# A vision tower in float32: the first attention in one block, another order in two linear attentions, and six picks in place of seven in the graph attention

## The chip, the cores and the metric

The kernel runs on one core of one Trainium2 chip. The metric is the device time of one launch, in microseconds (us). TensorE (PE) multiplies matrices, VectorE (DVE), ScalarE (ACT) and GpSimd (POOL) work on tiles, SyncE (SP) issues most transfers; GpSimd issues the indexed ones.

## The reference

A tower of ten parts in float32 works on `h`, 128 images of 64 tokens with 64 features: a token stage of Fourier layers, then four times an attention and an expert stage, each added to its input. Four parts matter here:

```python
# L0 attention, per image (64 tokens), on n = layernorm(h)
q = n @ q_weight; h = h + sigmoid(q @ n.T) @ n
# L2 attention: linear attention with 8 heads, then a small network, two layernorms
q, k, v = split(x @ Wqkv.T); q, k = elu(q) + 1, elu(k) + 1
out = (q @ (k.T @ v)) / (q @ k.sum() + 1e-6)     # per head
y = ln(out + x, g1, b1); h = h + ln(y + gelu(y @ W1 + b1) @ W2 + b2, g2, b2)
# L3 attention: the same linear attention on rmsnorm(x), one output product
# L3 experts: a graph attention over 262144 edges and 8192 loops decides the gate:
e = leaky_relu(a_src[src] + a_dst[dst]); alpha = segment_softmax(e, dst)
agg = segment_sum(h[src] * alpha, dst)
```

## The kernel before

`h` stays in SBUF as 64 tiles of 128 tokens. The program is a chain of stages, `t.stage(...)`: each is a block in which every engine has its own list of instructions, tied by semaphores, with a barrier of all engines behind it. Within a stage an engine works strictly in the order of its list; that order is written out by hand.

**First attention** (`l0_attention`). A loop of 4 rounds of 16 tiles; a round is three stages: `norm_stage` (mean, square, root, scaling on VectorE and ScalarE), `turn_stage` (TensorE turns the tiles, ScalarE copies them to `a_xt`) and a stage with query product, scores, sigmoid, values and the add to `h`, in groups of 4 tiles. Two images share a tile, so scores are 128 x 128 of which two quarters are used; the other two quarters of `a_att` are set to zero once in a stage of their own (L864).

**Linear attentions** (`l2_attention`, `l3_attention`). One stage each over 8 chunks of 8 tiles, in steps `s`. A step works on several chunks at once: L2 normalizes chunk s+1 (a), works out the attention of chunk s, the first norm of s-1 (b) and the second of s-2 (d). A chunk has two halves (`g` = 0, 1) of 4 tiles. On TensorE: `sums` (key times value, 8 small products of 64 rows), `outs` (query times the masked sums), `turn`, `features` (query, key and value), `hidden`, `dense`. `masked` on VectorE moves sums to `a_r`, from one bank that both halves share; `divide` takes `outs`. All turned tiles and `hidden` go through one bank, each copied by ScalarE before the next. In L2 VectorE adds the dense result (`add_dense`, L1670) right after the means of the other two chunks, and one scaling, one root and one reciprocal serve all three norms.

**Graph attention** (`graph_attention`). The edges, sorted by target, lie as 128 rows of 2112 columns, in 33 chunks of 64 columns. For each column 128 rows of a table of 8192 nodes (24 numbers) are needed. 36 columns (`ASKED`) are fetched by GpSimd, one indirect DMA each (L2779, `g_g`). The other 28 (`TURNED`) are picked by TensorE: 7 picks (`PICKS`) of 4 columns, each 16 products of a one-hot matrix `g_hot` with the table in SBUF. VectorE (L2835) and ScalarE (L2807, L2811) build `g_hot` from `g_near`, which SyncE loads; VectorE multiplies the result with a mask (L2850, `g_prod`) and reduces it (L2854). `hot_near` runs two picks ahead. Once a chunk `own_scores` completes the picked columns, and VectorE waits for the gathers of the chunk (its first reader is `g_a`, L2878) and works through scans up to `g_st`; in between it takes the first pick of the next chunk. GpSimd has three buffers and waits for `st_ready` (L2911) of the chunk three back. The stage before, `graph_table`, makes the table and the `near` and `far` numbers of the picked columns; the stage behind reads the states by 64 more gathers (L2961).

```python
for c in range(CHUNKS_E):
    if c >= GB: p.wait_ge(st_ready, c - GB + 1)
    for j in range(ASKED): p.indirect_dma_start(...)   # GpSimd
```

Of the kernel before, what the change touches and what calls it, by code (L numbers as in the profile page):

```python
# [8 lines left out]
ALU = mybir.AluOpType  # L9
# [3 lines left out]
P = 128  # L13
# [782 lines left out]
def norm_stage(t, src, dst, eps, centre=True, gain=None, shift=None, add_src=False):  # L796

    nc, n = t.nc, src.shape[1]
    mean, var, tmp = t.n_mean[:, 0:n], t.n_var[:, 0:n], t.n_tmp[:, 0:n, :]
    with t.stage("own", "centred", "squared", "var_ready", "std_ready") as (block, own, centred, squared, var_ready, std_ready):  # L800
        base = dst if centre else src

        @block.vector
        def _(v):
            c = Chain(v, own)
            if centre:
                c.link(v.tensor_reduce(mean, src, AX, ALU.add))
                c.link(v.tensor_scalar(mean, mean, -1.0 / D, None, ALU.mult))
                v.tensor_tensor(dst, src, bc(mean, D), ALU.add).then_inc(centred, 1)
            v.wait_ge(squared, 1)  # L810
            c.link(v.tensor_reduce(var, tmp, AX, ALU.add))
            v.tensor_scalar(var, var, 1.0 / D, eps, ALU.mult, ALU.add).then_inc(var_ready, 1)
            v.wait_ge(std_ready, 1)
            c.link(v.reciprocal(mean, var))
            c.link(v.tensor_tensor(dst, base, bc(mean, D), ALU.mult))
            if gain is not None:
                c.link(v.tensor_tensor(dst, dst, gain.unsqueeze(1).broadcast_to([P, n, D]), ALU.mult))
            if shift is not None:
                c.link(v.tensor_tensor(dst, dst, shift.unsqueeze(1).broadcast_to([P, n, D]), ALU.add))
            if add_src:  # L820
                c.link(v.tensor_tensor(dst, dst, src, ALU.add))

        @block.scalar
        def _(act):
            if centre:
                act.wait_ge(centred, 1)
            act.activation(tmp, base, ACT.Square).then_inc(squared, 1)
            act.wait_ge(var_ready, 1)
            act.activation(var, var, ACT.Sqrt).then_inc(std_ready, 1)

def turn_stage(t, src, dst):

    nc = t.nc
    with t.stage("turned", "moved") as (block, turned, moved):
        G = src.shape[1] // GT

        @block.tensor
        def _(pe):
            for g in range(G):  # L840
                if g >= 2:
                    pe.wait_ge(moved, g - 1)
                for k in range(GT):
                    last = pe.transpose(t.bank[g % 2][0:D, k * P:(k + 1) * P], src[:, g * GT + k, :], t.ident[:, :])
                last.then_inc(turned, 1)

        @block.scalar
        def _(act):
            for g in range(G):
                act.wait_ge(turned, g + 1)  # L850
                act.activation(dst[0:D, g * 512:(g + 1) * 512], t.bank[g % 2][0:D, :], ACT.Copy).then_inc(moved, 1)

def l0_attention(t, q_w):
    nc = t.nc
    with ExitStack() as ctx:
        x = t.sb("a0_x", [P, IT, D], ctx=ctx)
        xt = t.sb("a0_xt", [D + 1, IT * P], ctx=ctx)
        qt = t.sb("a0_qt", [D, 2, 512], ctx=ctx)
        att = t.sb("a0_att", [P, 2, GT, P], ctx=ctx)  # L860
        with t.stage("z") as (block, z):
            @block.vector
            def _(v):
                v.memset(att[:], 0.0)  # L864
        with nc.Fori(0, STEPS) as it:
            h = t.h[:, bass.ds(it * IT, IT), :]
            norm_stage(t, h, x[:], 1e-5)
            turn_stage(t, x, xt)
            with t.stage("q_done", "q_moved", "s_done", "a_ready", "v_done", "h_added") as (block, q_done, q_moved, s_done, a_ready, v_done, h_added):
                @block.tensor  # L870
                def _(pe):
                    def values(g):
                        pe.wait_ge(a_ready, g + 1)
                        if g >= 2:
                            pe.wait_ge(h_added, g - 1)
                        for k in range(GT):
                            last = pe.matmul(t.bank[4 + g % 2][:, k * D:(k + 1) * D], att[:, g % 2, k, :], x[:, g * GT + k, :], start=True, stop=True)
                        last.then_inc(v_done, 1)
                    for g in range(G):
                        if g >= 2:  # L880
                            pe.wait_ge(q_moved, g - 1)
                        pe.matmul(t.bank[g % 2][0:D, :], q_w, xt[0:D, g * 512:(g + 1) * 512], start=True, stop=True).then_inc(q_done, 1)
                        pe.wait_ge(q_moved, g + 1)
                        if g >= 2:
                            pe.wait_ge(a_ready, g - 1)
# [2388 lines left out]
```

## Time and profile before

| what | us |
|---|---|
| median of 3 runs | 11217.74 (11216.36 to 11220.24) |
| the profiled execution | 11220.0 |
| its span | 11218.2 |

### The profile page before, as it was taken

To read this page: it belongs to the slowest core of one execution; us is meant where nothing else is said; L and a number is where in the kernel's file an instruction comes from. 1 tells how busy PE (TensorE), PEld (TensorE's weight loads), DVE (VectorE), ACT (ScalarE), POOL (GpSimd) and SP (SyncE) were. 2 spreads that over 40 slices of the span, in tenths; PEclk is the share of its full clock that TensorE was granted. 3 is DMA by queue.
4 is the path that set the end of the run, shared out by engine and by line. 5 is a ranking of instruction groups with operands and counts; after the bars stand their busy time and mean duration, and the time that the engine had idled before them with its cause. 6 is when DMAs were issued, how large, how long until landed. Compare 5 with 4: busy or idle time off the path is not lost. (4 is left out here: it accounts for less than half of the span.)

```text
span 11218.2 us, 158703 instructions
## 1 busy us (share of the span) xinstructions
PE 9046.3 (81%) x63076; PEld 5585.6 (50%) x63076; DVE 7150.8 (64%) x9529; ACT 4551.4 (41%) x10565; POOL 5436.7 (48%) x5545
## 2 busy tenths in 40 slices
PE   4999899899996299469788888887667599999956
PEld 3666566566654266242222222223433477777742
DVE  5878788800000589734599999993444388888863
ACT  1333333333342133223477777872333233333322
POOL 0001777777777300037655555556164376666630
PEclk7999899989998699759999999997577599999977
DMA  5000100100010000000000000000000232222210
GB/s 183 20 20 21 33 22 23 29 27 22 21 37 17 27 21 4 28 12 1 1 2 2 2 2 2 2 2 1 1 1 1 26 57 56 55 55 55 53 55 8
DMA packets 274391, 281.84 MB, mean 25 GB/s; under 512 B 203241, under 2 KB 227573, under 8 KB 267832
## 3 DMA queue, kind: packets, MB, share of 16 engines
q1 hardware_dynamic: 96344, 251.64, 6.9%
q0 software_dynamic: 177312, 20.11, 3.2%
q8 instruction: 497, 8.14, 0.3%
q14 instruction: 238, 1.95, 0.1%
HBM read 210.30 MB, written 61.06 MB: 24 GB/s over the span
## 5 line engine op out<-in xcount | busy, mean ns | idle before, releaser
L2414 POOL DMA_INDIRECT sorted<-by_row_rows,by_row_idx x2112 | 2051.3, 971 | 2758.3 <-SPq L62 1176.3
L2500 POOL DMA_INDIRECT sorted<-r_rows,r_pos x2112 | 2054.2, 973 | 1705.5 <-PE bank L597 1063.1
L2080 DVE TENSOR_TENSOR a_top<-bank,a_k 128x2048 f32<-128x2048 f32 x896 | 1972.5, 2278 | 7.8 <-ACT a_qs L2135 6.9
L2795 PE MATMUL bank<-g_tab,g_hot 128*128 128x256 f32 x7392 | 1680.8, 391 | 234.8 <-DVE g_hot L2835 130.7
L2795 PEld LDWEIGHTS bank<-g_tab,g_hot 128*128 128x128 f32 x7392 | 1448.6, 197 | 466.7 <-DVE g_hot L2835 202.4
L2779 POOL DMA_INDIRECT g_g<-table,g_el x1188 | 1184.4, 997 | 580.8 <-issue 355.0
L578 PE MATMUL bank<-f_space,f_proj 128*128 128x512 f32 x2048 | 982.1, 603 | 386.8 <-DVE f_qa L780 384.4
L2282 PE MATMUL bank<-a_top,sc_pick_row 128*32 128x512 f32 x7168 | 951.9, 615 | 307.9 <-DVE a_top L2080 292.0
L2489 DVE TENSOR_TENSOR_SCAN r_work<-r_hit,r_base 128x528 f32<-128x528 bf16 x772 | 1017.1, 1317 | 27.6
L2128 ACT ACTIVATE a_over<-a_k,a_qs 128x64 f32<-128x64 f32 x4096 | 1021.3, 337 | 0.0
L780 DVE TENSOR_TENSOR f_qa<-f_qa,bank 128x512 f32<-128x512 f32 x128 | 82.2, 683 | 1469.5 <-PE bank L587 1275.0
L597 PE MATMUL bank<-f_space,f_to_y 112*128 112x512 f32 x2048 | 967.7, 600 | 19.7 <-ACT f_space L689 19.7
L704 ACT ACTIVATE f_space<-bank,f_b1r 128x512 f32<-128x512 f32 x1024 | 647.4, 683 | 821.6 <-PE bank L597 821.6
L587 PEld LDWEIGHTS bank<-f_from_y,f_space 128*128 128x128 f32 x6144 | 747.1, 192 | 185.1 <-issue 185.1
L578 PEld LDWEIGHTS bank<-f_space,f_proj 128*128 128x128 f32 x2048 | 388.6, 192 | 864.6 <-issue 829.6
L587 PE MATMUL bank<-f_from_y,f_space 128*128 128x96 f32 x6144 | 738.4, 273 | 0.0
L1365 DVE TENSOR_TENSOR e_hid<-e_hid,bank 128x512 f32<-128x512 f32 x512 | 338.5, 684 | 539.8 <-ACT e_hid L1328 214.1
L695 ACT ACTIVATE f_space<-bank 128x384 f32<-128x384 f32 x384 | 188.2, 490 | 1184.1 <-PE bank L587 1184.1
L2850 DVE TENSOR_TENSOR g_prod<-bank,g_mask 128x512 f32<-128x512 f32 x462 | 438.0, 1025 | 339.8 <-PE bank L2795 339.8
L2807 ACT ACTIVATE g_apart<-g_near,sc_place 128x512 f32<-128x512 f32 x462 | 308.0, 713 | 774.4 <-DMA g_near<-near 412.3
L2282 PEld LDWEIGHTS bank<-a_top,sc_pick_row 128*32 128x32 f32 x7168 | 151.0, 109 | 880.5 <-DVE a_top L2080 761.1
L2491 DVE COPY_PREDICATED r_work<-r_hit,r_work 128x528 f32<-128x528 uint16 x772 | 573.6, 743 | 0.0
(574 smaller groups left out, 13449.1 us busy)
## 6 DMA issues: line engine op xcount, KB each, us to landing
f_wm<-folded SPq DMA_DIRECT2D x16, 4608.0 KB
g_near<-near SPq DMA_DIRECT2D x231, 256.0 KB, 6.7
sorted<-r_rows,r_pos POOLq DMA_INDIRECT x2112
sorted<-by_row_rows,by_row_idx POOLq DMA_INDIRECT x2112, 2.1
states<-g_st SPq DMA_DIRECT2D x33, 768.0 KB, 3.8
g_g<-table,g_el POOLq DMA_INDIRECT x1188, 2.6
fp_raw<-t_modes SPq DMA_DIRECT2D x4, 2304.0 KB, 15.1
folded<-fp_turned SPq DMA_DIRECT2D x16, 576.0 KB, 9.2
```

Source lines behind the costliest of these rows:

```text
L578: last = pe.matmul(t.bank[4 + hf][:, :], proj[:, cg].rearrange("p o y -> p (o y)"), rr[:, cg % 2 * 2 + hf, :], start=(cg == 0), stop=(cg = ...
L587: last = pe.matmul(t.bank[6 + cg % 2][:, b * 96:(b + 1) * 96], rr[:, cg % 2 * 2 + hf, b * P:(b + 1) * P], const["from_y"][:, hf * 96:(hf + ...
L597: last = pe.matmul(t.bank[cg % 2 * 2 + hf][:, :], const["to_y"][:, hf * P:(hf + 1) * P], aa[:, cg, :], start=True, stop=True)
L704: last = act.activation(rr[:, cg % 2 * 2 + hf, :], t.bank[cg % 2 * 2 + hf][:, :], ACT.Relu, bias=f.b1r[:, u % LAYERS, cg:cg + 1])
L2080: v.tensor_tensor(top[:, n % RD].rearrange("p q (h s) -> p q h s", s=S), q, kk, ALU.max).then_inc(top_done, 1)
L2128: last = act.activation(over[:, slot, q, e, :], ks[:, k % 2, e, :], ACT.Relu, scale=-1.0, bias=qs[:, k % 2, slot, at_q:at_q + 1])
L2282: last = pe.matmul(sums[k % 2][32 * q:32 * q + 32, :], t.pick_row[:, i, :], rhs, start=False, stop=(i == I16 - 1), skip_group_check=True)
L2414: p.indirect_dma_start(out=self.dst, out_offset=bass.IndirectOffsetOnAxis(ap=self.idx[:, k:k + 1], axis=0), in_=self.rows[:, k, :], in_off ...
L2489: c.link(v.tensor_tensor_scan(self.run, self.hit[:], self.hit[:], self.base[:, i:i + 1], ALU.add, ALU.bypass))
L2500: p.indirect_dma_start(out=self.dst, out_offset=bass.IndirectOffsetOnAxis(ap=self.pos[:, k // PART_STEPS, at:at + 1], axis=0), in_=self.ro ...
L2779: p.indirect_dma_start(out=g[:, c % GB, j, :], out_offset=None, in_=d["table"], in_offset=bass.IndirectOffsetOnAxis(ap=el[:, at, 0:1], axi ...
L2795: last = pe.matmul(out, hot[:, n % HB, k, j * P:(j + 1) * P], by_near[:, k, :, 0:HD * EX], start=(k == 0), stop=(k == NEAR - 1))
```

## The change

The first attention becomes one stage over 8 chunks of 8 tiles. Each engine works on chunk s+1 (norm, turning) and chunk s (scores, sigmoid, values) in one step, and the products of the two images of a tile are made apart, as 64 x 64. The zero stage, the loop and the barriers go. In a step TensorE makes the scores of chunk s (16 products), turns both halves of chunk s+1 into two banks, makes the values of chunk s (16 products) and the query product of chunk s+1. ScalarE does the square of s+1, the sigmoid of s, the root of s+1 and two copies to `xt`. VectorE does two query copies of s, mean, scaling and centring of s+1, the add to `h` of s-1, then variance, reciprocal and scaling of s+1.

In the linear attentions both halves of `outs` follow `sums` before `features`, the turning of y (L2) or z (L3) of one half stands ahead of `features` and the other behind it. On VectorE in L2 the add of the dense result and its centring move behind `finish_q`, `finish_k` of half 0 ahead of the reduces; `masked(s, 1)` and `divide(s, 0)` move forward. `finish_k` waits for the value copies as well (`va_moved`).

In the graph attention `PICKS` is 6, so `TURNED` is 24 and `ASKED` 40.

```diff
 def l0_attention(t, q_w):
-        with nc.Fori(0, STEPS) as it:
-            norm_stage(t, h, x[:], 1e-5)
-            turn_stage(t, x, xt)
-            with t.stage("q_done", "q_moved", "s_done", ...):
+    CT, CG = 8, 2
+    NC8 = TILES // CT
+        with t.stage("own", "centred", "squared", ..., "h_added"):
+            @block.tensor
+            def _(pe):
+                for s in range(-1, NC8):
+                    if has(s):
+                        pe.wait_ge(q_moved, CG * (s + 1))
+                        if s >= 1:
+                            pe.wait_ge(a_ready, s)
+                        ...
+                    if has(s + 1):
+                        pe.wait_ge(x_ready, s + 2)
+                        ...
+                    if has(s):
+                        pe.wait_ge(a_ready, s + 1)
+                        ...
+                    if has(s + 1):
+                        ...
+            @block.scalar
+            def _(act):
+                ...
+            @block.vector
+            def _(v):
+                ...
@@ l2_attention, TensorE
                         pe.wait_ge(x_ready, s + 2)
-                        for g in range(CG):
-                            turn(x, 3, s + 1, g, n + g)
+                        turn(x, 3, s + 1, 0, n)
                     if has(s):
                         outs(s, 0)
                         sums(s, 1)
+                    if has(s + 1):
+                        turn(x, 3, s + 1, 1, n + 1)
+                    if has(s):
+                        outs(s, 1)
@@
                         turn(y, 2, s - 1, 1, m + 1)
-                    if has(s):
-                        outs(s, 1)
@@ l2_attention and l3_attention, VectorE
                     v.wait_ge(ex_k_done, CG * i + g + 1)
+                    v.wait_ge(va_moved, CG * i + g + 1)
@@ l2_attention, VectorE
-                    if has(d):
-                        add_dense(d)
-                        c.link(v.tensor_reduce(mean[:, 2], z[:, d % 3], AX, ALU.add))
-                    c.link(v.tensor_scalar(mean[:, lo:hi, :], mean[:, lo:hi, :], -1.0 / D, None, ALU.mult))
+                    if lo < 2:
+                        c.link(v.tensor_scalar(mean[:, lo:min(hi, 2), :], mean[:, lo:min(hi, 2), :], -1.0 / D, None, ALU.mult))
@@
+                    if has(s):
+                        finish_q(s)
                     if has(d):
+                        add_dense(d)
+                        c.link(v.tensor_reduce(mean[:, 2], z[:, d % 3], AX, ALU.add))
+                        c.link(v.tensor_scalar(mean[:, 2], mean[:, 2], -1.0 / D, None, ALU.mult))
                         v.tensor_tensor(c_[:], z[:, d % 3], bc(mean[:, 2], D), ALU.add).then_inc(centred, 1)
                     if has(s):
-                        finish_q(s)
+                        finish_k(s, 0)
@@
                     if has(s):
-                        for g in range(CG):
-                            finish_k(s, g)
+                        finish_k(s, 1)
@@ l3_attention, TensorE
+                        sums(s, 0)
+                        outs(s, 0)
+                        sums(s, 1)
                     if has(s + 1):
                         pe.wait_ge(y_ready, s + 2)
-                        for g in range(CG):
-                            turn(y, s + 1, g, n + g)
+                        turn(y, s + 1, 0, n)
+                    if has(s):
+                        outs(s, 1)
+                    if has(s + 1):
+                        turn(y, s + 1, 1, n + 1)
+                    if has(s):
+                        pe.wait_ge(o_used, CG * s + 1)
+                        turn(z, s, 0, m)
+                    if has(s + 1):
                         features(s + 1)
                     if has(s):
-                        outs(s, 1)
-                        for g in range(CG):
-                            pe.wait_ge(o_used, CG * s + g + 1)
-                            turn(z, s, g, m + g)
+                        pe.wait_ge(o_used, CG * s + 2)
+                        turn(z, s, 1, m + 1)
                         dense(s, m + 2)
@@ graph attention
-PICKS = 7
+PICKS = 6
```

## Rows read from the trace of the kernel before

**Rows 1.** Windows: us, busy PE, PEld, DVE, ACT, POOL, granted clock, DMA share, GB/s.

```profile
...
4754.00:4925.00 171.00, 105.59 (x352) 70.06 (x352) 40.52 (x61) 41.95 (x68) 0.00 (x0) 0.52 0.00 0
...
8930.00:10820.00 1890.00, 1681.41 (x7395) 1448.84 (x7395) 1500.57 (x2713) 595.80 (x991) 1185.01 (x1189) 0.95 0.27 54
```

**Rows 2.** Timeline, graph attention, one chunk: start, us, engine, line; [idle before <-releaser].

```profile
...
9803.47 44.68 PE L2795 MATMUL bank<-g_tab,g_hot 128*128 128x256 f32 x192 [4.07 <-DVE g_hot L2835]
...
9813.65 1.92 DVE L2850 TENSOR_TENSOR g_prod<-bank,g_mask 128x512 f32<-128x512 f32 x2 [2.34 <-PE bank L2795]
...
9820.56 1.91 DVE L2850 TENSOR_TENSOR g_prod<-bank,g_mask 128x512 f32<-128x512 f32 x2 [2.81 <-PE bank L2795]
...
9840.40 0.79 DVE L2878 TENSOR_TENSOR g_a<-g_g,g_flag 128x256 f32<-128x256 f32 x1
...
9849.61 7.14 PE L2795 MATMUL bank<-g_tab,g_hot 128*128 128x256 f32 x32 [1.46 <-issue]
```

**Rows 3.** Timeline, first and last chunk's g_a, and the next stage's start.

```profile
...
8991.61 0.79 DVE L2878 TENSOR_TENSOR g_a<-g_g,g_flag 128x256 f32<-128x256 f32 x1
...
10797.78 0.79 DVE L2878 TENSOR_TENSOR g_a<-g_g,g_flag 128x256 f32<-128x256 f32 x1
...
10819.34 0.79 SPq L2954 DMA_DIRECT2D k_x<-starts  x2
```

**Rows 4.** Windows of a busy stretch in L2 and of a slow pick.

```profile
...
8042.30:8053.50 11.20, 11.11 (x76) 8.21 (x78) 4.92 (x12) 1.51 (x3) 0.00 (x0) 0.50 0.00 0
9803.50:9808.50 5.00, 5.00 (x12) 4.01 (x13) 4.93 (x7) 0.00 (x0) 3.78 (x5) 0.50 0.78 214
```

**Rows 5.** Groups by line, graph attention, GpSimd: busy, mean ns, idle before.

```profile
...
L2779 POOL DMA_INDIRECT g_g<-table,g_el x1188 | 1184.4, 997 | 580.8 <-issue 355.0 <-DVEq L2911 225.7
```

**Rows 6.** Line L2779 alone: min/median/max ns, first and last start.

```profile
...
L2779 POOL DMA_INDIRECT g_g<-table,g_el x1188: 940/944/1467, 8930.9 to 10694.8; - x198
```

**Rows 7.** Timeline, GpSimd's first wait in the graph attention.

```profile
...
9407.36 1.19 POOL L2779 DMA_INDIRECT g_g<-table,g_el  x1 [8.89 <-DVEq L2911]
```

**Rows 8.** Timeline, first attention: start, a query product and copy, end.

```profile
...
4755.78 0.91 DVE L864 MEMSET a_att<- 128x1024 f32 x1 [57.51 <-PEq L70]
...
4783.02 1.97 PE L882 MATMUL bank<-a_xt,sw_a_q 64*64 64x512 f32 x2
...
4785.03 0.68 DVE L916 COPY a_qt<-bank 64x512 f32<-64x512 f32 x1 [1.36 <-PE bank L882]
...
4923.65 0.42 DVE L911 TENSOR_TENSOR h<-h,bank 128x256 f32 x1 [1.28 <-PE bank L877]
```

**Rows 9.** Timeline, second linear attention (L2), one chunk.

```profile
...
8038.77 0.18 DVE L1701 TENSOR_SCALAR a_var<-a_var 128x24 f32<-128x24 f32 x1
...
8044.43 1.11 PE L1536 MATMUL bank<-a_va,a_k 64*64 64x65 f32 x16
...
8045.48 1.06 PE L1506 MATMUL bank<-sc_ident,a_y 128*64 128x128 f32 x4
...
8059.48 1.28 ACT L1595 ACT_TABLE_LOAD   x1
...
8060.77 0.63 ACT L1595 ACTIVATE a_ex_q<-a_low_q 128x512 f32<-128x512 f32 x1
...
8063.30 0.69 DVE L1670 TENSOR_TENSOR a_z<-bank,a_y 128x512 f32<-128x512 f32 x1 [4.39 <-PE bank L1561]
...
8071.20 1.06 PE L1506 MATMUL bank<-sc_ident,a_x 128*64 128x128 f32 x4
...
8076.08 1.06 PE L1506 MATMUL bank<-sc_ident,a_y 128*64 128x128 f32 x4
```

**Rows 10.** Timeline, last linear attention (L3): dense products of two chunks.

```profile
...
8646.87 3.67 PE L1809 MATMUL bank<-sw_a_out,a_yt 65*128 65x64 f32 x16 [0.68 <-ACT a_yt L1867]
...
8670.61 3.67 PE L1809 MATMUL bank<-sw_a_out,a_yt 65*128 65x64 f32 x16 [0.68 <-ACT a_yt L1867]
```

**Rows 11.** Timeline, a gather of the stage after the graph attention.

```profile
...
10843.01 4.91 POOL L2961 DMA_INDIRECT k_se<-states,k_end  x1 [0.30 <-issue]
```

More of the change, by code:

```diff
@@ L793, in fno @@
         return f.h
[L796 to L829, printed above, removed]
@@ L832, in turn_stage @@
[L832 to L851, printed above, removed]
@@ new lines, in _ @@
+                c = Chain(v, own)
+                for s in range(-1, NC8 + 1):
+                    a, d = s + 1, s - 1
+                    if has(s):
+                        for g in range(CG):
+                            v.wait_ge(q_done, CG * s + g + 1)
+                            if s >= 2:
+                                v.wait_ge(s_done, s - 1)
+                            v.tensor_copy(qt[:, s % 2, g * 512:(g + 1) * 512], q_bank[g][0:D, :]).then_inc(q_moved, 1)
+                    if has(a):
+                        c.link(v.tensor_reduce(mean[:], chunk_of(a), AX, ALU.add))
+                        c.link(v.tensor_scalar(mean[:], mean[:], -1.0 / D, None, ALU.mult))
+                        v.tensor_tensor(x[:, a % 3], chunk_of(a), bc(mean[:], D), ALU.add).then_inc(centred, 1)
+                    if has(d):
+                        v.wait_ge(v_done, d + 1)
+                        v.tensor_tensor(chunk_of(d), chunk_of(d), v_bank[:, :].rearrange("p (j d) -> p j d", d=D), ALU.add).then_inc(h_added, 1)
+                    if has(a):
+                        v.wait_ge(squared, a + 1)
+                        c.link(v.tensor_reduce(var[:], sq[:], AX, ALU.add))
+                        v.tensor_scalar(var[:], var[:], 1.0 / D, 1e-5, ALU.mult, ALU.add).then_inc(var_ready, 1)
+                        v.wait_ge(std_ready, a + 1)
+                        c.link(v.reciprocal(mean[:], var[:]))
+                        v.tensor_tensor(x[:, a % 3], x[:, a % 3], bc(mean[:], D), ALU.mult).then_inc(x_ready, 1)
@@ L1574, in _ @@
                         sums(s, 1)
+                    if has(s + 1):
+                        turn(x, 3, s + 1, 1, n + 1)
+                    if has(s):
+                        outs(s, 1)
                     if has(s - 1):
@@ L1581, in _ @@
                         turn(y, 2, s - 1, 1, m + 1)
-                    if has(s):
-                        outs(s, 1)
-                    if has(s - 1):
                         for g in range(CG):
@@ L1708, in _ @@
                         v.tensor_tensor(x[:, a % 3], x[:, a % 3], bc(mean[:, 0], D), ALU.mult).then_inc(x_ready, 1)
+                    if has(s):
+                        masked(s, 0)
                     if has(b):
@@ L1714, in _ @@
                         v.sem_inc(y_ready, 1)
-                    if has(s):
-                        masked(s, 0)
                     if has(d):
                         c.link(v.tensor_tensor(c_[:], c_[:], bc(mean[:, 2], D), ALU.mult))
+                    if has(s):
+                        masked(s, 1)
+                        divide(s, 0)
+                    if has(d):
                         c.link(v.tensor_tensor(c_[:], c_[:], wide(g2), ALU.mult))
@@ L1956, in _ @@
                         v.sem_inc(y_ready, 1)
+                    if has(s):
+                        masked(s, 1)
+                        divide(s, 0)
                     if has(d):
@@ L1962, in _ @@
                     if has(s):
-                        masked(s, 1)
-                        for g in range(CG):
-                            divide(s, g)
+                        divide(s, 1)
 TILE_SENDS = 18
```

117 lines of the change are left out of this document (54 added, 63 removed).

## The prediction

> **What bounds the kernel now.** One core runs a chain of stages with a barrier after each, so what a stage loses or gains is lost or gained by the whole; the change touches four. I first took time, TensorE work and granted clock of the stages by windows [rows 1]: the first attention (171 us) and the graph attention (1890 us with its start and end) are shown. The reader is to see that TensorE is busy for 105.6 of 171 us in the first at a granted clock of 0.52, that is mostly 1.2 GHz, and 1681 of 1890 us in the second at 0.95, mostly 2.4 GHz. So the graph stage looks TensorE-bound, the first attention bound by a chain.
>
> Next one chunk of the graph attention in order of time [rows 2]. A pick (4 columns, 16 products) takes 6.91 us (two ends that VectorE's multiply follows: 9813.65 and 9820.56). Seven are 48.4 us. From the first chunk's processing to the last (`g_a`, 32 chunks on) it is 1806.17 us [rows 3], 56.44 us a chunk. The other 8 us are two pauses of TensorE, 4.07 and 1.46 us, in which VectorE works through its scans and builds no one-hot rows (after the first instruction of the scans, `g_a` at 9840.40, TensorE has no new rows until 9849.61), and a slow stretch behind the longer pause: from 9803.47 to 9813.65 a pick takes 10.2 us, 3.3 too much, while the granted clock is 0.50 [rows 4]; 48.4 + 5.5 + about 2.5 on average makes 56.4.
>
> Then GpSimd in that stage [rows 5]. Its 1188 gathers hold 1184.4 us and 355.0 us lie between them as issue: 1539.4 / 1188 = 1.296 us each, 36 of them 46.7 us. It has slack: the other idle time, 225.7 us, are waits of once a chunk until VectorE frees a buffer. Before the first of them it never waited: 360 gathers from 8930.9, the start of the first [rows 6], to 9407.36 less the 8.89 us of wait [rows 7] are 467.6 us, 1.299 each.
>
> **Change 1: 6 picks in place of 7.** It removes one pick a chunk, 6.91 us of TensorE, with two multiplies, a reduce and the one-hot rows on VectorE and ScalarE, which wait for TensorE there. VectorE and TensorE together would then need 56.44 - 6.91 = 49.5 us a chunk. It adds 4 gathers a chunk: 40 x 1.299 = 52.0 us. That is more than 49.5, so GpSimd becomes the bound. What stops for it is VectorE, at the first instruction that reads gathered rows (`g_a`), some 2.5 us a chunk; behind it are the scans, the exponentials and the one-hot rows of the third pick on, so TensorE's short pause grows from 1.5 to about 4 us. I also asked whether the pause costs a second slow stretch. It may (the pause of 4.07 us does), but then the processing needs up to 49.5 + 3.3 = 52.8 us, the wait for gathers vanishes and with it the longer pause. Both lie near 52, so I take 52.0.
>
> Bounds: from below 40 x (0.94 + 0.30), the least of a gather [rows 6] and its mean gap (355.0 / 1188), 49.6 us; from above 53.5, for a slow stretch in most chunks and a late landing.
>
> The stage: chunk 0 needs its 40 gathers, 8930.9 + 40 x 1.299 + 2.6 us to land = 8985.5, where `g_a` began at 8991.61. The last begins 32 x 52.0 later, 10649.5, and from it to the next stage are 21.6 us as before [rows 3]: 10671 in place of 10819.3, **148 us less** (225 less by the lower bound, 100 by the upper). The transfers of `g_near` fall from 231 to 198, with the same five in hand; those of `near` and the preparation of the table get shorter by a seventh in places where GpSimd's 64 other gathers and a slow store set the time, so I count nothing. SyncE's stores of the states stand behind fewer loads.
>
> **Change 2: the first attention as one pipeline.** Now the stage runs from 4755.78 to the end of the last add, 4924.07 [rows 8], 168.3 us, in four rounds of three blocks with barriers. The new one has 8 chunks of 8 tiles. Its loop closes over all engines, with prices from [rows 8, 9], from the start of a chunk's query product at 0: the first copy of it at 2.0 (as 4783.02 to 4785.03), the second after another 1.8, done at 4.5; three VectorE steps of the next chunk (mean, scale, centre: 0.6 + 0.2 + 0.7) to 6.0; square 0.65 on ScalarE to 6.7; table load 1.29 for the sigmoid to 8.0; sigmoid 0.65 to 8.65; table load for the root to 9.9; root 0.2, reciprocal and scaling to 11.1 with the handovers; on TensorE two turnings of 1.0 (to 13.1), the values as 16 small products at 1.05 per 8 (to 15.1); then the next query product. The scores, the add to h and the copies to `xt` lie beside it. So **15.1 us a chunk** at 1.2 GHz. Fill (norm, turn) about 6.8, drain (copies 4.5, scores 2.2, sigmoid 0.7, values 2.1, add 0.8) 10.3: 6.8 + 7 x 15.1 + 10.3 = 122.8 in place of 168.3: **45 us less**. The memset of `a_att`, its block and the zero halves of the products go with it. Bounds: 17 us a chunk if each of some ten handovers costs 0.2 us more than I give it (30 us gained), 11.4 if all of it ran at 2.4 GHz (below).
>
> Of the table load the row says that the next instruction starts 1.29 us after the load does, 8059.48 to 8060.77 [rows 9]. The Trainium skill, "ScalarE: Activation LUTs", section "What ACT_TABLE_LOAD costs", adds a drain of about 1.38 us to each switch, 2.66 in all. By the page two loads a chunk would make the chunk 17.8 us and the gain some 22 us smaller; the rows show no such drain here, and I go by them.
>
> **Change 3: second linear attention (L2), order of outputs.** One chunk takes 30.60 us (8045.48 to 8076.08), a closed chain in three parts [rows 9]: from the add of the dense result (8063.30) to the turning of x (8071.20) 7.90; from there to the turning of y 4.88; and from that turning through features and dense back to the add 17.82. The change moves that add behind the centring of x and y and `finish_q` (three steps at 0.6 leave the part), puts one `finish_k` (0.4) before the reduces, and lets the reciprocal wait for the root alone (0.3 less): 7.90 becomes 6.2. The second part gains one group of output products (1.05) and loses a wait for ScalarE's copy (0.75): 5.3 with a little wait for the second mask. In the third the copy of y is no longer hidden by those products, and they are gone: 17.5. Together 29.0, **1.6 less in each of 6 chunks and about 1 at the ends: 11 us**. VectorE gets lows earlier and has time for all of it. The added waits on `va_moved` cost nothing: ScalarE has both copies done 0.6 us after the exponentials, ahead of the squares that the variance needs; uncovered they would be 0.6 us a chunk. Bounds 0 and 20.
>
> **Change 4: the last linear attention (L3).** The dense products of one chunk and of the next start 23.74 us apart [rows 10]. The edit swaps two waits on copies (0.7 each) for one and puts the z turning ahead of the features, yet the dense product still stands behind features, two z turnings and a copy. By my count it saves 1.5 us at 1.2 GHz, but now and then TensorE has 2.4 GHz in the features, and a shift of that pattern eats as much. I take 0.5 a chunk, **4 us**; bounds -8 and +12.
>
> **The sum.** 148 + 45 + 11 + 4 = 208 us. The profiled execution took 11220.0 us (its span 11218.2 and 1.8 around it), 2.3 over the median 11217.74: 11220.0 - 208 = 11012 for such an execution, **11010** for the median. No change can be told from one within 0.2%, 22 us.
>
> **Rivals.** *A second slow stretch (0.17).* The pause that the gathers cause is added to the slow clock, and a chunk takes 53.5 us. For it: 4.07 us of pause is followed by a slow pick. Against: the two are coupled as above. Stage 100 us less, total 11058.
>
> *Gathers cheaper than they look (0.10).* The gathers that last longer than 0.94 lie beside VectorE's work, of which there is a seventh less in the picks. At 50.5 us a chunk 48 us more are gained: 10962.
>
> *The first attention at full clock (0.13).* In the new loop turning, values and query products stand back to back for 7.6 us. At 2.4 GHz the query copies come 1.8 us earlier, the turnings and values take half: 11.4 us a chunk, 30 us more: 10980. Against it: in the second linear attention TensorE is busy for 11.11 of 11.20 us and the clock stays at 0.50 all through [rows 4], with the same small products. The Trainium skill, "TensorE: Matmul & The Clock Gate", section "Part 1: The HAM clock gate", says that activity releases a throttled clock, which speaks for this rival; by that rule the row should have shown a rise, and it shows none.
>
> *Slower: gathers blocked (0.02).* In the next stage a gather lasts 4.91 us [rows 11], in a stretch in which VectorE runs steps over 4096 elements. If more gathers meant longer ones, the stage would turn: to be 22 us slower in spite of 60 us from the attentions, `g_a` must come every (10819.3 + 82 - 21.6 - 8985.5) / 32 = 59.2 us, 1.48 us a gather. The longest of 1188 is 1.467 and half of them last 0.94 [rows 6]; so hardly.
>
> *The change does little (0.03).* At 57 us a chunk (1.43 a gather) gains and loss cancel.
>
> **How the numbers follow.** The forecast has 0.55; its own range is 10985 to 11035, from 51.5 to 52.5 us a chunk and 10 us either way in the attentions. The range takes in the rivals with the slow stretch, the cheap gathers and the full clock but for their ends: 10955 to 11065. Only the last two rivals are not faster: faster 0.95, within 0.2% 0.03, slower 0.02.
>
> **What would show it.** In the graph stage: GpSimd without any wait for VectorE, `g_a` starting every 52 us with a wait for a gather of 2 to 3 us ahead of it, TensorE at some 1440 us of work with a larger idle share; `g_a` every 49.5 us, or GpSimd still waiting for VectorE, would show that GpSimd isn't the bound. In the first attention: sigmoids 15 us apart and two table loads a chunk. In the second linear attention: features 29.0 us apart. The prediction is wrong if the gathers change their price, or if the clock does.

## The result and the profile after

The changed kernel takes 10949.4 us (median of 4 runs, 10946.2 to 10952.9) against 11217.1 (4 runs, 11214.1 to 11220.2): a ratio of 0.9767, 95% interval 0.9755 to 0.9779, 268 us less. The forecast was 11010; the measured time lies 6 us under 10955, the low end of the range that was given. The profiled execution has a span of 10946.3 us, 271.9 less than before.

Anchors that stand in both programs cut the two spans into the same stages: the load of h, the first reduce of the experts, the memset ahead of L2, the reduce of the next experts, the memset ahead of L3, the first copy of the table, the first load of the graph attention and the first of the stage behind it. From the windows between them, in us:

| stage | before | after | measured | forecast |
|---|---|---|---|---|
| first attention, load included | 198.6 | 142.0 | -56.6 | -45 |
| second linear attention (L2) | 270.1 | 227.7 | -42.4 | -11 |
| last linear attention (L3) | 215.4 | 194.8 | -20.6 | -4 |
| preparation of the table | 132.4 | 129.2 | -3.2 | 0 |
| graph attention | 1890.3 | 1736.2 | -154.1 | -148 |
| all else | 8511.4 | 8516.4 | +5.0 | 0 |

Windows of the changed kernel: first attention, L2, L3 and graph attention (columns as in [rows 1]).

```profile
4728.50:4870.50 142.00, 63.51 (x608) 39.30 (x608) 41.54 (x80) 41.45 (x56) 0.00 (x0) 0.56 0.14 47
7850.50:8078.20 227.70, 139.71 (x992) 95.50 (x992) 155.33 (x324) 93.70 (x150) 0.00 (x0) 0.61 0.00 1
8487.10:8681.90 194.80, 125.00 (x960) 97.76 (x960) 121.26 (x301) 66.76 (x122) 0.00 (x0) 0.57 0.00 1
8811.10:10547.30 1736.20, 1458.13 (x6336) 1251.22 (x6337) 1350.59 (x2545) 513.64 (x859) 1310.03 (x1321) 0.93 0.29 55
```

The column to see is the granted clock. The same windows of the kernel before have 0.52, 0.51 and 0.52 in the three attentions: there TensorE ran at 1.2 GHz nearly throughout.

Groups of the changed kernel in the graph attention, GpSimd's gathers (answers to [rows 5]), and then the line of the first instruction that reads them: min/median/max ns, first and last start, and what its engine waited for.

```profile
L2764 POOL DMA_INDIRECT g_g<-table,g_el x1320 | 1309.1, 992 | 402.3 <-issue 402.3
```

```profile
L2863 DVE TENSOR_TENSOR g_a<-g_g,g_flag x33: 786/790/793, 8866.5 to 10525.7; 128x256 f32<-128x256 f32 x33
  DMA g_g<-table,g_el: 149.7, 32
```

(1309.1 + 402.3) / 1320 = 1.2965 us a gather, and GpSimd waits for nothing but its own issue: the waits for VectorE of [rows 5] are gone. `g_a` comes every (10525.7 - 8866.5) / 32 = 51.85 us, 40 gathers of 1.2965 to the hundredth, and waits 4.7 us for them each time.

Timeline of the changed kernel in the first attention: the scaling of three chunks, and one table load with the sigmoid behind it.

```profile
4770.39 1.28 ACT L861 ACT_TABLE_LOAD   x1
4771.68 0.60 ACT L861 ACTIVATE a_att<-bank 128x512 f32<-128x512 f32 x1
...
4774.07 0.69 DVE L895 TENSOR_TENSOR a_x<-a_x,a_mean 128x512 f32<-128x512 f32 x1
4787.59 0.69 DVE L895 TENSOR_TENSOR a_x<-a_x,a_mean 128x512 f32<-128x512 f32 x1
4802.17 0.69 DVE L895 TENSOR_TENSOR a_x<-a_x,a_mean 128x512 f32<-128x512 f32 x1
```

A chunk takes 14.58 us where its query product runs at 1.2 GHz (3.62 us) and 13.1 to 13.5 us where a part of it runs at 2.4 (2.2 to 2.6 us).

### The profile page after: what moved, and what is told of

Read it like the earlier page. It is cut to its first block and busy times, and to the rows that moved or that the text cites. A ratio compares the mean times of both kernels' runs of the same rounds, so it can differ in the third digit from the quotient of the medians.

```text
span 10946.3 us, 156350 instructions
## 1 busy us (share of the span) xinstructions
PE 8748.7 (80%) x62276; PEld 5333.8 (49%) x62276; DVE 7006.8 (64%) x9390; ACT 4467.7 (41%) x10421; POOL 5559.9 (51%) x5677
## 5 line engine op out<-in xcount | busy, mean ns | idle before, releaser
L2780 PE MATMUL bank<-g_tab,g_hot 128*128 128x256 f32 x6336 | 1458.1, 394 | 298.4 <-issue 181.1
L2764 POOL DMA_INDIRECT g_g<-table,g_el x1320 | 1309.1, 992 | 402.3 <-issue 402.3
L2780 PEld LDWEIGHTS bank<-g_tab,g_hot 128*128 128x128 f32 x6336 | 1251.2, 198 | 505.1 <-issue 193.0
L597 PEld LDWEIGHTS bank<-f_space,f_to_y 112*128 112x128 f32 x2048 | 364.7, 192 | 355.1 <-issue 328.6
L560 PE MATMUL bank<-f_to_x,f_bb 96*64 96x128 f32 (+1 forms) x4096 | 507.2, 289 | 31.2 <-ACT f_bb L684 31.2
```

Of the source, the lines that this page charges most:

```text
L597: last = pe.matmul(t.bank[cg % 2 * 2 + hf][:, :], const["to_y"][:, hf * P:(hf + 1) * P], aa[:, cg, :], start=True, stop=True)
L2764: p.indirect_dma_start(out=g[:, c % GB, j, :], out_offset=None, in_=d["table"], in_offset=bass.IndirectOffsetOnAxis(ap=el[:, at, 0:1], axi ...
L2780: last = pe.matmul(out, hot[:, n % HB, k, j * P:(j + 1) * P], by_near[:, k, :, 0:HD * EX], start=(k == 0), stop=(k == NEAR - 1))
```

## The experiments

Twelve runs, in three groups of four; those of one group ran on one chip. The kernel before took 11219.8 us on the first, 14970.5 on the second and 11199.2 on the third, and each ratio is against it on the same chip. On the second the stages with long runs of matmuls were longer, in every kernel (below), and the preparation of the table too (142 to 174 us). The first attention and L2 took the same time there as on the other chips, to 1 us; L3 did not always (185.5 us in e7 against 194.7 in e9, with the same code of L3). Only these three stages are read from it, L3 with that reserve.

### The parts alone

**e1: the picks**, in the kernel before, nothing else.

```
-PICKS = 7
+PICKS = 6
```

> The kernel before with only the six picks (24 of 64 edge columns picked by TensorE, 40 gathered); attentions as before. Theory A, GpSimd sets the chunk: its 40 gathers of 1.2965 us make g_a come every 51.9 us instead of 57.0, the graph attention falls by 154 us and the table by 3 us, the kernel to 11060 us. Theory B, the gain in the graph stage needs the earlier stages' new shape: less than 130 us. Nothing else moves by over 2 us under A.

Measured 11060.5 us, ratio 0.9865 (0.9848 to 0.9882); graph attention 1736.1. Theory A holds for that stage (the 57.0 us of the expectation should read 56.4). Yet L2, whose code is the old one, took 234.7 us instead of 270.1 in the profile. That execution took 11033.2 us, the other three of e1 11059.8 to 11074.9: L2's short time seems to be one of a single execution, not of the kernel.

**e2: the first attention.** The new function in the kernel before.

```
-def l0_attention(t, q_w):    # rounds of three blocks
+def l0_attention(t, q_w):    # one block, 8 chunks of 8 tiles
```

> The kernel before with only the new first attention. Theory A, the one block carries it: from the load of h to the first reduce of the experts 142 us instead of 198.5, chunks of 13.1 to 14.6 us depending on the granted clock, the kernel at 11161 us. Theory B, part of the 56 us came with the whole kernel's other edits: under 50 us.

Measured 11152.8 us, ratio 0.9943 (0.9921 to 0.9965); the stage took 141.8 us: theory A. L2, again the old code, took 245.2.

**e3: both linear attentions.** The kernel before with the edits of `l2_attention` and `l3_attention` alone; the two diffs of e5 and e6 below together.

> The kernel before with only the new orders of the two linear attentions. Order theory (the prediction's): L2 falls by 11 us and L3 by 4 to 11 us, as the order alone gives at a granted clock of 0.5, the kernel at about 11200 us. Clock theory: the new order also lets TensorE's granted clock rise to 1.0 in a part of every chunk, as in the changed kernel, so L2 falls by some 42 us (chunks of 24.1 instead of 30.6 us) and L3 by some 21 us, the kernel at 11157 us. Third possibility: the rises depend on how the stage's start happens to lie; then L2 and L3 come out between, and differently from the changed kernel.

Measured 11151.7 us, ratio 0.9942 (0.9925 to 0.9960); L2 228.7 and L3 194.7 us, as in the changed kernel. The clock theory's numbers came true.

Windows of L2 in e1, e2 and e3.

```profile
7910.30:8145.00 234.70, 132.65 (x992) 90.38 (x992) 152.41 (x316) 94.59 (x150) 0.00 (x0) 0.62 0.00 1
```

```profile
7853.10:8098.30 245.20, 143.33 (x992) 97.14 (x992) 152.44 (x317) 94.66 (x150) 0.00 (x0) 0.59 0.00 1
```

```profile
7910.40:8139.10 228.70, 140.38 (x992) 95.82 (x992) 155.34 (x323) 93.82 (x150) 0.00 (x0) 0.61 0.00 1
```

The same 992 matmuls of the same code hold 169.0 us of TensorE in the profile before and 132.7 in e1. The old order of L2 has two cycles: one of 30.61 us a chunk, in which the clock never rises, and one of 23.5 to 23.8 us. An execution can change between them: in e2 the first sums of successive chunks are 23.6, 23.8, 23.8, 25.9, 30.6 and 29.4 us apart, behind a first step of 21.2. TensorE in the kernel before, the dense products and the next chunk's first sums, and then in e1, the first sums of two successive chunks and what lies between.

```profile
8059.52 3.67 PE L1561 MATMUL bank<-sw_a_w,a_ft 65*128 65x64 f32 x16 [0.68 <-ACT a_ft L1624]
...
8069.94 1.13 PE L1536 MATMUL bank<-a_va,a_k 64*64 64x65 f32 x16 [6.75 <-DVE a_k L1647]
```

```profile
8025.51 1.13 PE L1536 MATMUL bank<-a_va,a_k 64*64 64x65 f32 x16 [6.75 <-DVE a_k L1647]
...
8033.49 2.05 PE L1524 MATMUL bank<-sw_a_kv,a_xt 64*128 64x128 f32 x16
...
8040.43 2.00 PE L1561 MATMUL bank<-sw_a_w,a_ft 65*128 65x64 f32 x16 [0.68 <-ACT a_ft L1624]
8049.18 1.13 PE L1536 MATMUL bank<-a_va,a_k 64*64 64x65 f32 x16 [6.75 <-DVE a_k L1647]
```

The pause ahead of the sums is as long as in the kernel before, 6.75 us; most of the matmuls in between take about half as long (the dense group 2.00 instead of 3.67). The chunk is 6.9 us shorter by the clock alone.

### Is it TensorE's pause, or its start?

**e4: the old order with the pause filled.**

```
 if has(s):
+    for _ in range(14):        # 7 in L3
+        pe.matmul(sum_bank[:, 260:388], t.ident[:, :], t.ident[:, :], start=True, stop=True, skip_group_check=True)
     sums(s, 0)
```

> The kernel before in its old order, with matmuls of the identity by itself into unused columns of the sums' bank put into TensorE's long pause of each chunk: 14 in L2 (about 6.6 us at a granted clock of 0.5, in a pause of 6.75 us) and 7 in L3 (3.3 us in 3.4 us). Clock theory: TensorE is granted 1.0 for most of L2 and L3, its work on the path halves, chunks go from 30.6 to 20 to 24 us and from 25.3 to 18 to 20 us, L2 falls by 40 to 70 us and L3 by 20 to 40 us without any change of order, the kernel at about 11130 us. Rival: the clock stays at 0.5 in the old order whatever TensorE does in the pause, and the time stays within 10 us of before or rises.

Measured 11198.0 us, ratio 0.9981 (0.9971 to 0.9991); L2 242.4, L3 210.9. The clock's mean in L2 rose to 0.70, and yet two of its chunks took 30.61 us. Windows of L2 in e4:

```profile
8022.00:8034.00 12.00, 11.28 (x83) 8.51 (x82) 4.89 (x13) 2.47 (x4) 0.00 (x0) 0.50 0.01 1
8034.00:8044.00 10.00, 8.64 (x27) 5.28 (x27) 5.18 (x11) 4.83 (x9) 0.00 (x0) 0.50 0.00 0
8046.00:8052.00 6.00, 2.64 (x32) 2.05 (x31) 5.90 (x12) 3.25 (x5) 0.00 (x0) 1.00 0.00 0
```

TensorE is busy for 19.9 of the 22 us from 8022 to 8044 at 0.50, and has the clock of 1.00 just behind, where it has 2.6 us of work in 6. Filling the pause moves the fast stretch about and partly puts it into the pause, where it earns nothing. So the clock theory as I had put it, that work in the pause is enough, is refuted for L2.

**e11: the old order with only the start filled**, in L2 and, ahead of `y_ready`, in L3.

```
 if has(s + 1):
+    for _ in range(16 if s < 0 else 0):
+        pe.matmul(sum_bank[:, 260:388], t.ident[:, :], t.ident[:, :], start=True, stop=True, skip_group_check=True)
     pe.wait_ge(x_ready, s + 2)
```

> The kernel before with 16 matmuls of the identity ahead of the first turning of L2 and of L3, nothing else. Theory of two cycles (what the clock does in the first chunks decides whether the old order settles at chunks of 23.7 us with a rise in each or at 30.6 us without): L2 falls from 270 to about 235 us, the kernel to 11180 us, and the spread of its times narrows. Rival: the cycle is left and entered at random on the way, and a start that is held at work changes nothing that lasts: L2 anywhere between 235 and 270 us.

Measured 11205.5 us, ratio 1.0005 (0.9991 to 1.0019). The profile has L2 at 231.7 us, but the ten runs spread from 11166.5 to 11228.5, no narrower than the kernel before (21 runs, 11171.1 to 11221.8), and the profiled one took 11175.8. By that spread the start does not decide the cycle; L2's time in the other nine was not seen. What decides it is open.

### Which engine's order

**e5: TensorE's new order alone** in both linear attentions, VectorE's as before. L2's part:

```
-    for g in range(CG):
-        turn(x, 3, s + 1, g, n + g)
+    turn(x, 3, s + 1, 0, n)
 if has(s):
     outs(s, 0)
     sums(s, 1)
+if has(s + 1):
+    turn(x, 3, s + 1, 1, n + 1)
+if has(s):
+    outs(s, 1)
 ...
-if has(s):
-    outs(s, 1)
```

> The kernel before with only TensorE's new order in the two linear attentions; VectorE's as before. The earlier runs gave for L2, old order, chunks of 30.6 us with the granted clock at 0.5 throughout and of 23.5 to 23.8 us with a rise to 1.0 in the chunk; for the new orders 23.7 to 24.4 us with a rise in every chunk; for L3 25.26 us against 23.67 us at 0.5 and 23.5 to 23.7 against 18.0 to 18.9 us with a rise. Theory 1, TensorE's order alone makes the new figures: L3's chunks at 0.5 take 23.7 us, and L2 has a rise in every chunk, 228 to 235 us in all. Theory 2, VectorE's order makes them (its reads stand ahead of the adds): L3 stays at 25.3 us at 0.5, L2 at 240 to 270 us.

L2 took 252.4 us, L3 220.3; as a whole 14965.1 us, ratio 0.9994 (0.9979 to 1.0008).

**e6 and e12: VectorE's new order alone**, TensorE's as before; e12 is e6 on the third chip. L2's part, cut:

```
-if has(d):
-    add_dense(d)
 ...
+if has(s):
+    finish_q(s)
+if has(d):
+    add_dense(d)
 ...
 if has(s):
-    masked(s, 1)
-    for g in range(CG):
-        divide(s, g)
+    divide(s, 1)
```

> The kernel before with only VectorE's new order in the two linear attentions; TensorE's as before. Theory 1 (TensorE's order makes the gain): L2 240 to 270 us with chunks of 30.6 us where the clock stays at 0.5, L3 near 214 us. Theory 2 (VectorE's order makes it): L2 near 228 us, L3 near 195 us.

> The kernel before with VectorE's new order alone in the linear attentions, once more. If that order makes the rise of L2's clock in every chunk (e6: chunks of 23.25 to 23.90 us, L2 227.6 us) and not the chip or chance: L2 at 228 us again and L3 at 213 to 218 us, so the kernel at 11175 us. If e6 was chance, L2 comes out between 235 and 270 us.

e6: 14961.1 us, ratio 1.0003 (0.9988 to 1.0017), L2 227.6, L3 218.3. e12: 11175.6 us, ratio 0.9983 (0.9972 to 0.9994), L2 227.7, L3 219.9. Theory 2 for L2, and for L3 neither. TensorE's line of the first sums, successive chunks of L2: first e5, then e12.

```profile
10629.75 1.13 PE L1536 MATMUL bank<-a_va,a_k 64*64 64x65 f32 x16 [6.75 <-DVE a_k L1647]
...
10633.88 1.23 PE L1549 MATMUL bank<-a_r,a_qt 64*64 64x72 f32 x16 [1.80 <-issue]
...
10658.12 1.13 PE L1536 MATMUL bank<-a_va,a_k 64*64 64x65 f32 x16 [6.75 <-DVE a_k L1647]
```

```profile
8014.49 1.13 PE L1536 MATMUL bank<-a_va,a_k 64*64 64x65 f32 x16 [2.88 <-DVE a_k L1648]
...
8022.56 1.06 PE L1506 MATMUL bank<-sc_ident,a_y 128*64 128x128 f32 x4
...
8031.84 3.68 PE L1561 MATMUL bank<-sw_a_w,a_ft 65*128 65x64 f32 x16 [0.68 <-ACT a_ft L1624]
8038.40 1.13 PE L1536 MATMUL bank<-a_va,a_k 64*64 64x65 f32 x16 [2.88 <-DVE a_k L1648]
```

With TensorE's order alone the pause of 6.75 us stays, a wait of 1.80 us comes behind the first turning, and most chunks take 28.0 to 28.4 us although the clock rises in them. With VectorE's alone the pause is 2.88 us, and every chunk but the first takes 23.3 to 23.9 us, in both runs. What that order is worth without the clock can be estimated from these rows: from the turning of y to the dense products e12 needs 9.28 us, the kernel before 14.04 (8045.48 in [rows 9] to 8059.52); 23.91 + 4.76 = 28.7 us a chunk, 1.9 under the 30.6 of before. The forecast had 1.6 for the whole edit. No profile shows L2 with the new order at a clock of 0.50 throughout.

In L3 the two orders together are needed: each alone took longer than the kernel before (220.3 and 218.3 to 219.9 us against 215.4), both together 194.7. A chunk at a clock of 0.50 throughout takes 25.26 us before and in e12, and 23.67 in the changed kernel; with a rise it takes 23.3 to 23.7 before and 18.0 to 18.9 in the changed kernel. Its first sums in three successive chunks:

```profile
8580.38 1.13 PE L1767 MATMUL bank<-a_va,a_k 64*64 64x65 f32 x16 [3.38 <-DVE a_k L1874]
...
8598.40 1.13 PE L1767 MATMUL bank<-a_va,a_k 64*64 64x65 f32 x16 [3.74 <-DVE a_k L1874]
...
8617.30 1.13 PE L1767 MATMUL bank<-a_va,a_k 64*64 64x65 f32 x16 [3.37 <-DVE a_k L1874]
```

### The price of a gather

**e7 and e9: five picks** in the changed kernel (20 columns picked, 44 gathered), on the second and the third chip.

```
-PICKS = 6
+PICKS = 5
```

> The changed kernel with five picks instead of six (20 of 64 edge columns picked, 44 gathered). Theory A, GpSimd sets the chunk with 1.2965 us a gather: 44 gathers make 57.0 us a chunk, the graph attention takes 1736 + 33 times 5.19 = 1907 us, slower than the kernel before's 1890, and the whole kernel 11120 us. Rival, TensorE or the clock set it: TensorE's work falls by another eighth, and the stage takes less than 1736 us. L2 and L3 are untouched here and show again whether the new orders always come out at 228 and 195 us.

> The changed kernel with five picks (44 gathers a chunk) once more, since e7's chip gave every kernel with long stretches of matmuls a third more time, the kernel before included (14,970 us), and there TensorE's own work set the graph stage. On a chip like that of the first runs, GpSimd theory: 44 gathers of 1.2965 us make 57.0 us a chunk, the graph attention takes 1907 us against the changed kernel's 1736, the kernel about 11120 us. Rival, TensorE sets it here too: under 1736 us.

e9: 11110.0 us, ratio 0.9927 (0.9912 to 0.9943), graph attention 1898.1 us. Its lines of the gathers and of `g_a`:

```profile
L2764 POOL DMA_INDIRECT g_g<-table,g_el x1452 | 1430.9, 985 | 442.4 <-issue 442.4
```

```profile
L2863 DVE TENSOR_TENSOR g_a<-g_g,g_flag x33: 786/791/793, 8871.9 to 10689.2; 128x256 f32<-128x256 f32 x33
  DMA g_g<-table,g_el: 553.6, 33
```

(1430.9 + 442.4) / 1452 = 1.290 us a gather, `g_a` every 56.8 us = 44 x 1.290, behind a wait of 16.8 us. The stage is 9 us under the expected 1907, as a gather took 1.290 and not 1.2965 us. GpSimd sets the chunk; with seven picks it is the other engines (56.4), with six it is GpSimd by 4.7 us, with five it costs as much as one pick too many: 1890, 1736, 1898 us.

e7 on the second chip: 14529.4 us, ratio 0.9708 (0.9684 to 0.9732), and the rival's picture: with seven, six and five picks (e5, e8, e7) the graph attention took 2870, 2766 and 2536 us there. TensorE in that stage, first in the kernel before, then in e5, which has the same code:

```profile
L2795 PE MATMUL bank<-g_tab,g_hot 128*128 128x256 f32 x7392 | 1680.8, 391 | 234.8 <-DVE g_hot L2835 130.7 <-ACT g_hot L2811 58.8 <-issue 45.4
```

```profile
L2799 PE MATMUL bank<-g_tab,g_hot 128*128 128x256 f32 x7392 | 1950.7, 417 | 929.6 <-issue 738.9 <-DVE g_hot L2839 135.9 <-ACT g_hot L2815 44.1
```

The matmuls are 7% longer, and 739 us of idle time stand ahead of them that no wait explains, at a granted clock of 0.78 instead of 0.95. Of the three numbers of picks the least is the best on that chip.

### More of the faster clock

**e8: the changed kernel with its pauses filled** by the line of e4, its result used by nothing. In the first attention, and the others likewise (8 in L2 and 7 in L3 ahead of `sums(s, 0)`; 16 ahead of the first turning of each):

```
+for _ in range(11):
+    pe.matmul(t.bank[6][:, 0:128], t.ident[:, :], t.ident[:, :], start=True, stop=True, skip_group_check=True)
 pe.wait_ge(x_ready, s + 2)
```

> The changed kernel with matmuls of the identity by itself put into TensorE's pauses, results unused: in the first attention 11 ahead of each wait for a centred chunk (pauses of 4.6 to 5.4 us), in L2 8 and in L3 7 ahead of the first sums of a chunk (pauses of 2.9 and 3.4 us), and 16 ahead of the first chunk of each. Clock theory: more of the three stages runs at a granted clock of 1.0; the first attention falls from 142 to 120 to 130 us (chunks of 11.4 instead of 13.7 us), L2 from 228 to 205 us, L3 from 195 to 180 us, the kernel to about 10900 us. Rival: a chunk's length is held by chains through ScalarE and VectorE, or the fillers at 0.5 stand in the way of the sums; then no gain, or up to 20 us lost.

14733.0 us, ratio 0.9848 (0.9827 to 0.9869). First attention 128.1 us, as the clock theory has it. L2 took 235.3 us, 7 us longer than unfilled (e7 228.0): the rival there. L3 took 180.9 us, but e7, on the same chip and unfilled, took 185.5, with a rise in five of its chunks instead of three:

```profile
11230.10:11415.60 185.50, 115.66 (x960) 91.08 (x960) 121.29 (x301) 66.79 (x122) 0.00 (x0) 0.61 0.00 1
```

**e10: filled where e8 gained.** Against e8, in L2:

```
-for _ in range(8):
-    pe.matmul(sum_bank[:, 260:388], t.ident[:, :], t.ident[:, :], start=True, stop=True, skip_group_check=True)
 sums(s, 0)
```

> The changed kernel with matmuls whose results nothing uses only where e8 showed a gain: 11 ahead of each wait for a centred chunk in the first attention, 16 ahead of L2's first turning, 16 ahead of L3's first turning and 7 ahead of L3's first sums of each chunk. Clock theory, from e8's stages: the first attention 128 us (before 142), L2 224 us, L3 181 to 190 us (195), the kernel at 10920 to 10930 us, below the changed kernel's 10949. Rival: the fillers' gain in e8 belonged to its chip; the time stays at 10949 us.

10911.1 us (five runs, 10895.5 to 10932.8), ratio 0.9758 (0.9742 to 0.9774). The windows of the first attention, L2, L3 and the graph attention:

```profile
4726.50:4854.60 128.10, 75.03 (x784) 57.41 (x784) 41.57 (x81) 40.95 (x56) 0.00 (x0) 0.77 0.16 52
7834.70:8059.00 224.30, 140.76 (x1024) 98.67 (x1024) 155.31 (x323) 93.74 (x150) 0.00 (x0) 0.64 0.00 1
8464.70:8634.80 170.10, 123.94 (x1104) 103.39 (x1104) 120.94 (x301) 66.55 (x122) 0.00 (x0) 0.75 0.00 1
8764.60:10499.90 1735.30, 1456.22 (x6336) 1250.18 (x6337) 1351.18 (x2545) 513.64 (x859) 1309.19 (x1321) 0.93 0.28 55
```

Against the changed kernel 13.9, 3.4 and 24.7 us less in the three attentions. The first attention's gain is shown: 128.1 us in e8 and e10, 141.8 to 142.0 in the four profiles of the same code unfilled (after, e2, e7, e9). In L2 the 3.4 us are hardly more than the scatter of the unfilled stage (227.7 to 230.6 in after, e3, e7 and e9). In L3 e8 has the very code of e10 and took 180.9 us, and the unfilled stage lies between 185.5 and 194.8, so how much of the 24.7 us the fillers make isn't shown; the profiled execution was also the fastest of the five. All five runs lie under the lowest of the changed kernel, 10946.2, but the two were timed on different chips and the intervals of their ratios overlap, so a gain of the whole kernel isn't shown.

## Why the prediction was right, and where it wasn't

**The picks: right.** GpSimd became the bound at 51.85 us a chunk (forecast 52.0), without a wait for VectorE, TensorE with 1458 us of work (1440), the stage 154 us less (148). The wait ahead of `g_a` is 4.7 us, not 2 to 3: without it a chunk would take some 47.2 us (51.85 - 4.7, an estimate) and not 49.5. TensorE's line in the changed kernel shows why:

```profile
9767.82 34.80 PE L2780 MATMUL bank<-g_tab,g_hot 128*128 128x256 f32 x160 [2.46 <-DVE g_hot L2820]
9808.33 10.17 PE L2780 MATMUL bank<-g_tab,g_hot 128*128 128x256 f32 x32 [5.71 <-issue]
9819.52 34.80 PE L2780 MATMUL bank<-g_tab,g_hot 128*128 128x256 f32 x160 [1.02 <-DVE g_hot L2820]
```

The short pause grew from 1.46 to 5.71 us, as forecast in kind (about 4), and the slow pick (10.17 us) now stands behind it, beside VectorE's scans, where VectorE does not wait for it; the pause behind the scans shrank from 4.07 us to between 1.0 and 2.5, and the picks that VectorE does wait for are fast (34.80 / 5 = 6.96 us). So the slow stretch was not doubled, as the first rival had it: it moved to where it costs the chunk little. By the prediction's own 3.3 us for it, 49.5 - 3.3 = 46.2 would be left without the wait. Both figures are estimates, since the wait is what moved the slow stretch. Chunks of 53.5 or of 50.5 us did not come, and no gather got dearer.

**The first attention: the mechanism right, the clock mis-sized.** The closed loop and its two table loads are there. From the first query product to the last it is 13.9 us a chunk instead of 15.1, 8 us in all, and the drain is 7.5 us instead of 10.3. A chunk whose TensorE work is at 1.2 GHz takes 14.58, so 0.5 us of the difference is the sum's and 0.7 the clock's. The rival with the full clock had 11.4; e10 comes to 12.1 with its pauses filled. The Trainium skill, "TensorE: Matmul & The Clock Gate", section "Part 1: The HAM clock gate", from which that rival drew support, has the throttled clock as the default, released by activity. The trace agrees here (with more work the mean clock is 0.77 and not 0.56) and disagrees in L2 (e4: 19.9 of 22 us busy at 0.50). The Trainium skill, "ScalarE: Activation LUTs", section "What ACT_TABLE_LOAD costs", has a drain of about 1.38 us behind each table load of a switch. It is absent from this trace too: the sigmoid starts 1.29 us after its table load does (4770.39 to 4771.68).

**L2: the step that failed** is "Together 29.0": it priced every part at the clock that one profile showed, as if a granted clock of 0.50 belonged to the stage. It belonged to one of two cycles. At that clock VectorE's part of the edit would be worth about what was forecast for the whole (1.9 us a chunk by the estimate above, 1.6 forecast); no run shows it. In the fast cycle the old order's chunk is no longer than the new one's (23.5 to 23.8 against 24.1 us), and only the way to the second chunk's sums is shorter, by 7 us (20.0 + 15.1 in e3 against 21.0 + 21.2). That way, from the first chunk's sums to the second's, in the kernel before (e1 has the same 21.2 us) and in the changed one:

```profile
7926.39 1.13 PE L1536 MATMUL bank<-a_va,a_k 64*64 64x65 f32 x16 [3.95 <-DVE a_k L1647]
...
7934.08 3.78 PE L1524 MATMUL bank<-sw_a_kv,a_xt 64*128 64x128 f32 x16
...
7947.55 1.13 PE L1536 MATMUL bank<-a_va,a_k 64*64 64x65 f32 x16 [8.54 <-DVE a_k L1647]
```

```profile
7870.49 1.13 PE L1510 MATMUL bank<-a_va,a_k 64*64 64x65 f32 x16 [2.98 <-DVE a_k L1622]
...
7878.13 2.05 PE L1498 MATMUL bank<-sw_a_kv,a_xt 64*128 64x128 f32 x16
...
7885.20 1.13 PE L1510 MATMUL bank<-a_va,a_k 64*64 64x65 f32 x16 [5.02 <-DVE a_k L1622]
```

Even there a part is the clock: the key and value product takes 2.05 us and not 3.78, 1.7 of the 7 us.

What the edit does beyond that: in all seven profiles with VectorE's new order and L2's pauses unfilled (after, e3, e6, e7, e9, e10, e12) the stage is in the fast cycle, 224 to 231 us, where the old order gave 270 (before), 245 (e2), 235 (e1) and 232 (e11). Why VectorE's order brings the rise so reliably isn't settled. So of the 42 us some 35 are the other cycle (270.1 against 234.7 in e1), and the last 7 are order and clock together. Against a luckier execution of the kernel before the same change would be worth less. But the 268 us do not rest on one unlucky execution: the four runs of the kernel before lie within 6.1 us, and its medians on the first and the third chip are 11219.8 and 11199.2. Whether the new orders make the times steadier is not shown: the kernel before spreads over 36 us (13 runs) and 51 us (21 runs), e9 over 4.4 (4 runs), e3 over 16 (4 runs), e12 over 24 (10 runs).

**L3: the same step.** "a shift of that pattern eats as much" had the sign wrong. The order alone saves 1.59 us a chunk at 0.50 (forecast 1.5), and three of seven chunks (18.0, 18.9, 18.2) have a long rise and save 5 more, where a rise saved 1.7 before. How many chunks have one varies: five in e7, and the stage took 185.5 us there.

**The table: counted at nothing, rightly.** The kernels with seven picks (e2 to e4, e11, e12) have it at 129.1 to 130.7 us too; 132.4 before was that execution's.

The range was too narrow because its bounds for L2 and L3 (0 to 20, -8 to 12) were made at one clock. With L2 as it was measured in the other cycle the sum would have been 10979, and with L3's rise 10962.

## What to carry to other kernels

Where the granted clock stands at 0.50 in a short pipelined stage, price each edit at both clocks, and profile the unchanged stage several times before its time is believed: in the profile of e1, with an edit elsewhere, it was 35 us shorter. Count all engines' pace per chunk before taking work off one of them: the gain ends at the next one's, here 4.7 us away. Filling TensorE's pauses is worth trying stage by stage, since it gave 14 us in one stage on two chips, between 5 and 25 in a second whose own time varies by 9, and took 7 in a third.

## What was not expected of the hardware

- TensorE's clock in L2, whose chunks take 24 to 31 us, runs in a cycle with a rise in every chunk or in one without any, at the same work, and can change from one to the other within the stage (e2). Filling the pause did not keep the chunks short (e4: two of 30.61 us).
- One chip of three ran stretches of dense matmuls so that the kernel before took 14970 us instead of 11200: experts and inner attention 4030 instead of 2980 us, graph attention 2870 instead of 1890, with 739 us of idle time of TensorE there that no wait explains. The preparation of the table, with 45 to 47 us of TensorE work, took 142 to 174 instead of 129 to 132, while the first attention took the same (198.7 against 198.6). What held TensorE back there is open. It turned the ranking of seven, six and five picks round.
- A gather of 128 rows costs GpSimd 1.29 to 1.30 us of its time whether 36, 40 or 44 stand in a chunk, of which 0.99 on average is the instruction and 0.30 the issue.
